# Moving half of a plane's wipes ahead of a SELU stage, and splitting its LayerNorm statistics in two steps, in a four-layer graph network on one core

## The reference, cut to what matters

```
x = layernorm(x + L0(x))   # graph attention, 8 heads, softmax over a node's edges, + bias, SELU
x = layernorm(x + L1(x))   # three times: h = x + segment_sum(x[src], dst); x = relu(relu(h @ wa + ba) @ wb + bb)
x = layernorm(x + L2(x))   # graph attention, 4 heads, self loops, skip product, own LayerNorm
x = layernorm(x + L3(x))   # three graph convolutions with edge weights and degree normalisation
```

## Time and profile before

| | us |
|---|---|
| median of 3 runs | 6158.92 |
| lowest and highest | 6153.66, 6160.87 |
| profiled execution, own time | 6153.7 |
| its span | 6153.7 |
| busy: PE / DVE / ACT / POOL | 3502.0 / 2931.0 / 1698.2 / 3308.1 |
| POOL's scatters (L838), 1568 | 1618.2 busy, 490.4 idle before them |

### The profile page before, as it was taken

One profiled execution on the slowest core, in us unless ns is written; L12 is line 12 of the kernel. 1 busy time (PEld: TensorE's weight loads), 2 busy tenths in 40 slices (PEclk: granted clock), 3 DMA queues, 4 the chain that ended last, 5 costly groups with the idle time before them and its releaser, 6 DMA issues. The chain is left out here.

```text
span 6153.7 us, 43187 instructions
## 1 busy us (share of the span) xinstructions
PE 3502.0 (57%) x13009; PEld 2055.1 (33%) x13009; DVE 2931.0 (48%) x6509; ACT 1698.2 (28%) x2011; POOL 3308.1 (54%) x3349
## 2 busy tenths in 40 slices
PE   3000000050097789999999211111099999999999
PEld 2000000010043347777777100010054445444444
DVE  4766666669656664556564455555560000000111
ACT  2443343121010005666677333333240000000000
POOL 5777777577777777777775677777610000000000
PEclk7555555565598899999999555555599999999999
DMA  4566565399953443344478333333378888888887
GB/s 147 192 220 217 212 221 202 103 363 367 341 176 98 132 130 114 114 117 123 138 231 256 99 122 111 114 119 111 129 232 283 295 295 296 291 295 299 291 303 264
DMA packets 509068, 1255.63 MB, mean 204 GB/s; under 512 B 114559, under 2 KB 164197, under 8 KB 500133
## 3 DMA queue, kind: packets, MB, share of 16 engines
q1 hardware_dynamic: 387860, 1126.44, 53.8%
q0 software_dynamic: 119952, 125.65, 8.2%
q10 hardware_dynamic: 1024, 0.79, 0.0%
HBM read 873.83 MB, written 378.71 MB: 204 GB/s over the span
## 5 line engine op out<-in xcount | busy, mean ns | idle before, releaser
L838 POOL DMA_INDIRECT plane<-total,cell x1568 | 1618.2, 1032 | 490.4 <-issue 427.3
L470 POOL DMA_INDIRECT gb<-rows,src x1564 | 1488.1, 951 | 526.0 <-issue 475.1
L1014 PE MATMUL psum<-gb,big 128*128 128x512 f32 (+1 forms) x3822 | 1585.1, 569 | 2.8 <-DVE turned L1198 2.3
L1014 PEld LDWEIGHTS psum<-gb,big 128*128 128x128 f32 x3822 | 693.5, 191 | 766.6 <-issue 765.5
L1415 PE MATMUL psum<-gb,row_part 128*128 128x512 f16 x1911 | 420.3, 373 | 473.6 <-DMA gb<-plane 473.6
L2489 ACT COPY gb<-turned 128x1632 f32<-128x1632 f32 (+3 forms) x138 | 450.8, 3267 | 722.7 <-DVE turned L2584 722.7
L2510 PE MATMUL psum<-identity,end_top 128*8 128x128 f32 (+1 forms) x2 | 0.7, 374 | 1084.1 <-DVE end_top L2590 1084.1
L1415 PE MATMUL psum<-strips,ring 128*128 128x512 f32 (+1 forms) x2548 | 609.7, 394 | 13.5 <-issue 7.5
L1435 ACT CAST strips<-gb 128x1024 fp32r<-128x1024 f16 (+1 forms) x529 | 559.4, 1075 | 126.8 <-DMA gb<-plane 38.2
L2878 PE MATMUL psum<-w_L_gnn_skip_W,turned 128*128 128x128 f32 x98 | 39.0, 502 | 848.0 <-ACT turned L2896 848.0
L2584 DVE TENSOR_TENSOR_SCAN turned<-gb,psum 128x1632 f32<-128x1632 f32 (+3 forms) x138 | 457.8, 3317 | 68.6 <-ACT gb L2471 66.0
(11 more groups left out here) (420 smaller groups left out, 4649.0 us busy)
## 6 DMA issues: line engine op xcount, KB each, us to landing
gb<-plane SPq DMA_DIRECT2D x588, 512.0 KB, 4.4
gb<-plane SPq DMA_DIRECT2D x294, 576.0 KB, 4.8
plane<-turned SPq DMA_DIRECT2D x49, 3200.0 KB, 28.5
gb<-plane SPq DMA_DIRECT2D x588, 256.0 KB, 3.1
gb<-plane SPq DMA_DIRECT2D x294, 288.0 KB, 3.3
plane<-turned SPq DMA_DIRECT2D x49, 1600.0 KB, 10.9
runs<-gb SPq DMA_DIRECT2D x33, 1748.0 KB, 6.1
runs<-gb SPq DMA_DIRECT2D x33, 1610.0 KB, 5.7
```

The source lines that it names most:

```text
L470: m.s_rows[b % BUFS].up(nc.gpsimd.indirect_dma_start(m.batch(b, columns, row)[:, j, 0:width], None, table, bass.IndirectOffsetOnAxis(ap=m. ...
L838: done.up(m.nc.gpsimd.indirect_dma_start(plane, bass.IndirectOffsetOnAxis(ap=m.cell[:, r:r + 1], axis=0), total[:, r:r + 1], None), 16)
L1014: mm = nc.tensor.matmul(m.psum[:, self.bank(r, 0, i), 0:nodes], rows, slot[:, a:a + nodes], start=(s == 0), stop=False)
```

## The change

Three things are edited.

- Wipes: during attention 1 SP also wipes the first 24 tiles of plane 1, behind those of plane 0 of the same batch, and `Selu.sp` wipes the other 25.
- Kept rows: SP's one store of x is replaced by 13 stores, one for each quad, that ACT issues when it has normalised the quad.
- Statistics: `statistics` no longer makes the reciprocal and the shift; those are in a new step `shifts`. ACT's square root moves from `normal` to a new step `deviation`, which is issued one quad ahead. On DVE the quads now come one to a unit: behind unit k (from 0) come the split of quad k-2, the shifts of quad k-1 and the statistics of quad k. The small tiles have four places in place of two.

```diff
                 if head.first and b:
                     wipe(m, sp, 0, wiped_by(b - 1, batches), wiped_by(b, batches))
+                    wipe(m, sp, 1, wiped_by(b - 1, batches) // 2, wiped_by(b, batches) // 2)
...
     def scratch(self, g):
-        part = self.far[:, g % 2 * 64:(g % 2 + 1) * 64]
+        part = self.far[:, g % 4 * 64:(g % 4 + 1) * 64]
...
+    def deviation(self, act, g):
+        m = self.m
+        tiles = tiles_of(g)
+        _, pairs, root, _ = self.scratch(g)
+        act.wait_ge(m.s_var.sem, m.s_var.at(tiles[-1] + 1))
+        m.s_root.up(m.nc.scalar.activation(root[:, 0:len(tiles)], pairs[:, 0:len(tiles), 1], ACT.Sqrt, bias=self.eps))
+
     def normal(self, act, g):
...
-        act.wait_ge(m.s_var.sem, m.s_var.at(tiles[-1] + 1))
-        m.s_root.up(nc.scalar.activation(root[:, 0:n], pairs[:, 0:n, 1], ACT.Sqrt, bias=self.eps))
...
+    def keep(self, act, g):
+        m, t = self.m, self.quad(g)
+        act.wait_ge(m.s_normal_kept.sem, m.s_normal_kept.at(g + 1))
+        m.s_kept.up(act.dma_start(by_tile(m.kept)[:, t, :], self.x[:, t, :]), 16)
...
+        self.deviation(act, 0)
         for g in range(QUADS):
+            if g + 1 < QUADS:
+                self.deviation(act, g + 1)
             self.normal(act, g)
-        act.wait_ge(m.s_kept.sem, m.s_kept.at(16))
+            self.keep(act, g)
+        act.wait_ge(m.s_kept.sem, m.s_kept.at(16 * QUADS))
...
-        if g >= 2:
-            dve.wait_ge(m.s_normal.sem, m.s_normal.at(tiles_of(g - 2)[-1] + 1))
+        if g >= 4:
+            dve.wait_ge(m.s_normal.sem, m.s_normal.at(tiles_of(g - 4)[-1] + 1))
...
+    def shifts(self, dve, c, g):
+        m, nc = self.m, self.m.nc
+        n = len(tiles_of(g))
+        _, pairs, root, shift = self.scratch(g)
+        dve.wait_ge(m.s_var.sem, m.s_var.at(tiles_of(g)[-1] + 1))
         dve.wait_ge(m.s_root.sem, m.s_root.at(g + 1))
         c.link(nc.vector.reciprocal(root[:, 0:n], root[:, 0:n]))
...
-        behind = {3 + 3 * g // 2: g for g in range(QUADS)}
...
-            if k in behind:
-                self.statistics(dve, c, behind[k])
-            if k - 2 in behind:
-                self.split(dve, c, behind[k - 2])
+            if 0 <= k - 2 < QUADS:
+                self.split(dve, c, k - 2)
+            if 0 <= k - 1 < QUADS:
+                self.shifts(dve, c, k - 1)
+            if k < QUADS:
+                self.statistics(dve, c, k)
...
-        wipe(m, sp, 1, 0, TILES)
-        sp.wait_ge(m.s_normal_kept.sem, m.s_normal_kept.at(QUADS))
-        m.s_kept.up(sp.dma_start(by_tile(m.kept), self.x), 16)
+        wipe(m, sp, 1, TILES // 2, TILES)
```

More of the change, by code:

```diff
@@ L2748, in normal @@
         n = len(tiles)
-        _, pairs, root, shift = self.scratch(g)
-        act.wait_ge(m.s_var.sem, m.s_var.at(tiles[-1] + 1))
-        m.s_root.up(nc.scalar.activation(root[:, 0:n], pairs[:, 0:n, 1], ACT.Sqrt, bias=self.eps))
+        _, _, root, shift = self.scratch(g)
         act.wait_ge(m.s_stats.sem, m.s_stats.at(g + 1))
@@ L2800, in statistics @@
         n = len(tiles)
-        stats, pairs, root, shift = self.scratch(g)
+        stats, pairs, _, _ = self.scratch(g)
         dve.wait_ge(m.s_joined_kept.sem, m.s_joined_kept.at(g + 1))
-        if g >= 2:
-            dve.wait_ge(m.s_normal.sem, m.s_normal.at(tiles_of(g - 2)[-1] + 1))
+        if g >= 4:
+            dve.wait_ge(m.s_normal.sem, m.s_normal.at(tiles_of(g - 4)[-1] + 1))
         for k, t in enumerate(tiles):
@@ L2828, in dve @@
         c.link(m.nc.vector.tensor_copy(m.step_bank, m.step_pairs))
-        behind = {3 + 3 * g // 2: g for g in range(QUADS)}
-        assert len(UNITS) > max(behind) + 2
+        assert len(UNITS) > QUADS + 2
         self.degrees(dve, c)
```

## The result

The changed kernel takes 6177.93 us as the median of six executions; one of them, 8667 us at a granted clock of 0.742, is disturbed and left out of the ratio, and the other five lie between 6173.35 and 6182.62 with a median of 6177.03. The kernel before took 6158.49 in six (6153.66 to 6160.87). The ratio is 1.0033, 95% interval 1.0022 to 1.0044: slower by 0.33%, with a forecast of 6177.6. The profiled execution has a span of 6174.9 us and an own time of 6177.0. Span against span it is 21.2 us more, median against median 19.4, or 18.5 with the median of the five. (An execution's own time stands some 2 us above its span in every run that has both. The table ahead of the prediction had set the two equal, so the profiled execution before need not be the fastest of the three, as it said.)

What follows compares the result with a forecast made beforehand. GpSimd's chain of scatters, through its ticks, was taken to set layer 1's end; 0 (attention 1) + 0 (rows earlier) + 18.7 (GpSimd stands) on the median 6158.9 gave 6177.6 us, range 6160 to 6205.

Steps and rivals of the forecast that it cites:

- Rows earlier = 0: Start of layer 1: TensorE's first round comes 147 us earlier, near 1558, worth 0 since rounds three to six await ticks.
- Attention 1 = 0: Attention 1: the 24 added wipes fit in the DMA bandwidth and cost GpSimd's gathers 0 us.
- the forecast's own sign: Attention 1: the prediction is wrong if, among other signs, this stage's last store is later than before.
- The cover: Attention 1: 25 us between a store's landing and GpSimd's need of that buffer, to absorb delays from wipes.
- VectorE's stand, and GpSimd's: SELU stage: VectorE waits some 66 us behind unit 2 for ScalarE's root; GpSimd stands 18.7 us before unit 3.
- Once, and not again: After unit 3: GpSimd stands only once, as units 4 to 7 are ready before GpSimd wants them.
- The thin margins: Units 4 to 6: ready only 2.8 to 4 us early; a split costing 3 us more would add a few us.
- What follows from the ticks: Layer 1 onward: last tick near 2245, last round's end near 2333, everything after later by 18.7 us.
- no change: Rival, 0.10: 6159, VectorE's stand doesn't reach GpSimd, given a root by 1309.7 or a reserve 15 scatters larger.
- Faster: Rival, 0.05: the rows set the end of layer 1, TensorE starts 185 us earlier, 5974.
- The gathers starve: Rival, 0.09 in full or part: attention 1's wipes delay gathers, 72 us on top of 18.7, about 6250.

Runs made afterwards that it cites:

- the kernel three units later: The changed kernel with each quad's statistics, shifts and split three units later, the root's wait behind unit 5: 6160.59 us, 1.0004 of the kernel before.

## Why the prediction was right

**Rows earlier = 0: right.** TensorE's first round came at 1559.0 (forecast 1558), 146 us earlier, released by the second tick at 1555.48. The copies started at 1506.52 (1508). Three kernels with starts at 1540.9, 1617.9 and 1704.8 end layer 1 at 2314.6, 2314.4 and 2312.8.

**Attention 1 = 0: off by some 3 us, and by the forecast's own sign wrong.** The cover held in the middle of the stage, and the gathers kept their pace. What was missed is the stage's end, where the last gathers already wait for a store, so there is no cover left; the working looked at a batch in the middle only. It costs 2.6 us of waiting. The forecast was to be wrong if attention 1's last store came later, and it does: SP's next issue behind the stores (L2457 in before, L2458 in the changed kernel) is at 1118.63 and not at 1115.36, and over the six profiled executions at 1118.4 to 1118.6 with the wipes and 1115.4 to 1116.7 without. Up to the SELU stage other differences blur this: in the changed kernel's execution the 15th scatter was 4.3 us later than in the earlier trace rows; over the profiled executions it stands at 1232.2, 1232.8 and 1233.6 without the wipes, and at 1233.5, 1235.7 and 1237.0 with them.

**VectorE's stand, and GpSimd's: right.** Forecast 66 and 18.7 us; measured 65.1 and 17.9 in the kernel with the order alone, 63.3 and 15.5 in the changed one. The latter is smaller since GpSimd was through with its cells 4.3 us later while the root came only 0.4 us later: from the 15th scatter to ScalarE's table load it was 90.3 us (1237.04 to 1327.37) in this execution and 92.7 to 94.2 in the five others. Unit 3 starts 1341.41 − 1321.93 = 19.5 us later all the same, where the forecast had 18.7. So two terms were off in opposite directions (some 3 to 4 us and −3 us), and that the sum came out to the microsecond, the tick at 2245.67 against a forecast of 2245 and the median within 1 us of 6177.6, is luck.

**Once, and not again: right.** The thin margins held, each unit where it was put. Last steps of units 4 to 7 were forecast at 1354.7, 1371.2, 1388.9 and 1400; in the trace they start at 1354.95, 1371.27, 1388.81 and 1399.87, and GpSimd's last wait of over 1 us for VectorE's cells is that of unit 3. Units 5 to 7 were put by an estimate with no rows beside it, so that they fell within 0.2 us of it is in part luck too.

**What follows from the ticks: right.** Last tick +19.3 us, layer 1's end +19.9 (2332.7), layer 2's first matmul +19.9 (2339.4 against 2319.5). The remaining 1 to 2 us of the spans' 21.2 lie behind it, within what executions of one kernel differ (6153.7 to 6160.9). One place where the profiled executions differ is the matmuls on `strips,high`, which take 355.2 us in before (3043.9 to 3399.1) and 356.8 to 363.6 us in the other five, whichever way their ticks moved; why is not explained.

The rivals: "no change" falls with the gap at 1341.41; the kernel three units later shows that its condition, a larger reserve of cells when the wait comes, makes it true. "Faster" falls with three starts and one end. "The gathers starve" falls with 81 gathers in 100 us, except for the 2.6 us above.

What stays open: whether the place of the wait alone, with the statistics in one step, costs the same where the ticks set layer 1's end (tried only on a chip where they don't); what the kept rows do alone on a chip of the first kind; and why the changed order gains 0.4 to 0.95% on the other chips. The last tick doesn't explain that gain: with the order alone it is 2535.0 and with the wipes alone 2528.2, and yet layer 1 ends at 3042.6 and 3095.5. The start of layer 1 goes with it: the three kernels with the new order start it at 1776.2, 1789.0 and 1823.8 and end it at 3025.7, 3032.1 and 3042.6, the five others start at 1902.8 to 1929.6 and end at 3051.7 to 3096.7. So the rival "the rows set the end of layer 1", false on the first kind, may hold in part where TensorE's own pace fills layer 1. No run changed the start alone there, so this is argued and not shown.

## What to carry to other kernels

A wait put into a busy engine's queue costs what stands behind it, less what its consumer still holds in reserve: find when the awaited value can be ready at all, count the consumer's reserve in time up to there (here 70 scatters of 1.27 us), and put the wait behind the work that fills the rest. An early transfer or an early start, even of 146 us on the busiest engine, is worth nothing if a later stage is released by a chain on another engine; look for the last such release before the stage's end and ask whether the change moves that. Look for cover at the end of a stage too, not only in its middle. And read in a trace of the chip that is measured which chain sets the stage's end: on another chip of the same type it was another one here.

## What the hardware showed unexpectedly

VectorE slows GpSimd's indirect DMAs, by form of operand. Beside L815, whose two tensor inputs both lie in SBUF, a scatter's time rose from 0.97 us up to 1.60 as VectorE's instructions grew to some 1 us; until 2181 us it stays 0.97 us in the kernel where L815 begins only then. Length is not it: L752 is the same operation with its second tensor in PSUM, takes 1.03 us at its longest and runs back to back from 2112 to 2122 us, and the eight scatters beside it there take 0.96 to 0.99 us. Two rows of before, and one of the kernel with the later L815 at the time of the first:

```profile
2159.13 1.36 POOL L838 DMA_INDIRECT plane<-total,cell  x1 [0.30 <-issue]
2194.89 1.60 POOL L838 DMA_INDIRECT plane<-total,cell  x1 [0.30 <-issue]
```

```profile
2158.76 0.96 POOL L838 DMA_INDIRECT plane<-total,cell  x1 [0.30 <-issue]
```

The Trainium skill, "SBUF — State Buffer", section "Who interferes with whom", says that a VectorE instruction with two SBUF inputs contends with a GpSimd instruction that reads SBUF. The trace agrees, if a scatter's issue is taken as such a reader (its cells and values lie in SBUF): beside L815 it is slowed and beside L752 it is not. From 2140 to 2218 us the mean scatter takes 1.15 us in before and 1.02 in the kernel with the later L815 (61.85 / 54 and 59.95 / 59), and the tick there comes 7.5 us earlier.

Busier DMA engines delay the landing of an indirect DMA (a gather's from 2.6 to 6.7 us when the share went from 0.61 to 0.79, a scatter's from 2.2 to 6.6 us) and don't slow its issue: 80 and 81 gathers in 100 us.

Chips of one type differ by 15%: 6157 us and 7106 to 7112 us for the same kernel, with idle times of about 1 us between VectorE's short instructions and of up to 3.2 us between TensorE's matmuls on the slower ones. What makes them so is not known. The same edit, the order alone, is 0.3% slower on the one kind and 0.4% faster on the other.
